# One mLSTM head stage on TensorE, with and without the filler products between its heads

## The reference

```python
D = exp(log_D - max_log_D)                # log_D: sums of log forget gates + input gate, -inf above the diagonal
C = (q @ k.T) / sqrt(32) * D
h = C / (max(|sum(C)|, exp(-max_log_D)) + 1e-6) @ v
```

## Time and profile before

| | |
|---|---|
| median of 3 runs | 1674.55 us |
| profiled execution | 1677.74 us |
| its span, first to last instruction | 1676.0 us |
| mean granted TensorE clock | 0.901 |
| heads: first to last `weigh` | 88.1 to 267.7 us |
| TensorE, VectorE busy, whole span | 1346.0, 1241.5 us |

### The profile page before, as it was taken

One profiled execution on the slowest core, in us unless ns is written; L12 is line 12 of the kernel. 1 busy time (PEld: TensorE's weight loads), 2 busy tenths in 40 slices (PEclk: granted clock), 3 DMA queues, 4 the chain that ended last, 5 costly groups with the idle time before them and its releaser, 6 DMA issues. The chain is left out here.

```text
span 1676.0 us, 24635 instructions
## 1 busy us (share of the span) xinstructions
PE 1346.0 (80%) x8976; PEld 758.8 (45%) x9000; DVE 1241.5 (74%) x1952; ACT 767.8 (46%) x1451; POOL 325.5 (19%) x233
## 2 busy tenths in 40 slices
PE   5599993636868989873967759679999999999996
PEld 3378773212334444432645546334444444444443
DVE  5567777825558778956999999488877777887764
ACT  3445562715334444424978879323333334433322
POOL 0032424607445557531000000000000000000000
PEclk8789996558888999996979889789999999999998
DMA  8312231355142242226030000000000000000000
GB/s 290 117 52 61 102 101 41 128 147 157 55 131 83 90 124 88 101 67 247 3 125 0 25 0 0 1 1 7 6 6 13 6 6 6 6 6 9 10 6 13
DMA packets 56493, 102.17 MB, mean 61 GB/s; under 512 B 9823, under 2 KB 20727, under 8 KB 56300
## 3 DMA queue, kind: packets, MB, share of 16 engines
q1 hardware_dynamic: 55148, 97.14, 17.5%
q0 software_dynamic: 1280, 4.20, 0.9%
HBM read 73.47 MB, written 27.66 MB: 60 GB/s over the span
## 5 line engine op out<-in xcount | busy, mean ns | idle before, releaser
L2084 PE MATMUL HG<-W1H,XT 128*128 128x512 f16 x512 | 166.6, 387 | 27.2 <-ACT XT L2045 20.7
L1558 PE MATMUL FD<-W0D,HH 128*128 128x512 f16 x512 | 159.6, 395 | 14.8 <-DMA W0D<-down_weights,IDX 12.2
L2084 PE MATMUL HU<-W1H,XT 128*128 128x512 f16 x512 | 163.2, 380 | 0.0
L2110 PE MATMUL HD<-W1H,HT 128*128 128x512 f16 x512 | 155.2, 380 | 0.0
L1552 PE MATMUL FG<-F,W0G 97*128 97x512 f16 x324 | 86.1, 400 | 52.9 <-DMA F<-features_kept 24.5
L2053 ACT ACTIVATE SG<-HG,DS 128x512 f32<-128x512 f32 x64 | 43.9, 686 | 160.6 <-PE HU L2084 160.6
L1805 ACT ACTIVATE PR<-A_S,NM,CM 128x512 f32<-128x512 f32 x128 | 99.5, 777 | 34.2 <-DVE NM L1946 34.2
L2187 DVE SCALAR_TENSOR_TENSOR H<-HU,DS,SG 128x512 f32<-128x512 f32 x64 | 48.0, 750 | 87.6 <-ACT SG L2053 85.7
L1442 POOL TENSOR_TENSOR HL<-HM,HH 128x512 f16<-128x512 f32 x64 | 92.3, 1442 | 86.0 <-ACT HH L1481 85.5
L335 ACT ACTIVATE DD<-E,TM 128x128 f32<-128x128 f32 x256 | 72.7, 369 | 70.3 <-PE E L431 68.7
L1558 PE MATMUL FD<-W0D,HL 128*128 128x512 f16 x256 | 100.1, 391 | 0.0
(11 more groups left out here) (335 smaller groups left out, 3369.8 us busy)
## 6 DMA issues: line engine op xcount, KB each, us to landing
VALP<-in_ffn_weights_dram SPq DMA_DIRECT2D x24, 512.0 KB, 3.6
VALQ<-in_ffn_weights_dram SPq DMA_DIRECT2D x24, 512.0 KB, 3.6
quantised_weights<-QQ SPq DMA_DIRECT2D x24, 512.0 KB, 2.8
X<-in_x_dram SPq DMA_DIRECT2D x8, 1024.0 KB, 6.0
CTX<-in_ctx_dram SPq DMA_DIRECT2D x8, 1024.0 KB, 5.6
W1H<-quantised_weights SPq DMA_DIRECT2D x3, 2048.0 KB, 10.6
W1L<-quantised_weights SPq DMA_DIRECT2D x3, 2048.0 KB, 15.4
F<-features_kept SPq DMA_DIRECT2D x16, 288.0 KB
```

Of the source, the lines that this page charges most:

```text
L1558: last = pe.matmul(DN[c][:, :], lhs[:, i, c * P:(c + 1) * P], W2[:, i, part, :], start=(i == 0 and n == 0), stop=(i == KI - 1 and n == 2))
L2084: ins = pe.matmul(bank[:, :], lhs, rhs, start=(i == 0), stop=(i == len(terms) - 1))
L2110: ins = pe.matmul(DN[0][:, :], HT[:, q, lp, k, :], W[:, 2, i * D:(i + 1) * D], start=(i == 0 and lp == 0 and W is WH), stop=(i == KI - 1 a ...
```

## The change

The function `fill` and its five calls go, which are 73 filler products between the heads. The twelve in front of the first head stay, and so does everything else, the order of the other products included.

```diff
-            def fill(n):
-                if n < HEADS:
-                    if n >= 2:
-                        pe.wait_ge(d_ready, n - 1)
-                    keep_warm(1, E[n % 2])
-
             def decay(n):
...
                         i += 1
-                    if c == 2 and n:
-                        fill(HG * n + HG)
                 last.then_inc(state_ready, 1)
...
                 if pair % 2 == 0:
                     read_state(pair // 2)
-                    fill(ahead + 1)
                 if pair + 1 < HEADS // 2:
                     scores(pair + 1)
                 weigh(2 * pair + 1)
-                fill(ahead + 1)
                 decay(ahead + 1)
                 if pair % 2 == 1 and pair + 1 < HEADS // 2:
-                    fill(ahead + 2)
                     state(pair // 2 + 1)
```

## The result

The kernel after the change takes 1683.33 us, the median of 20 runs (1673.88 to 1704.36), against 1676.23 us for the kernel before (20 runs, 1672.37 to 1683.17). The ratio is 1.0044, 95% interval 1.0024 to 1.0063: 7.4 us slower, between 4 and 11. The forecast was 1685. Every ratio here compares whole sets of runs, lies near the quotient of their means and not of the medians (these differ by 7.1 us), and leaves out runs over 1.5% above the fastest of their kernel, which are one of the twenty after the change and three of the six of `rows32`.

What follows compares the result with a forecast made beforehand. TensorE, busy 80% of the span, and its granted clock were taken as the bounds. Direct saving -7.5 us and further clock falls +18 us gave +10.5 us on 1674.55, so 1685 us; range 1665 to 1712 us.

Steps and rivals of the forecast that it cites:

- 43 fillers are on its path, 30 in a wait: In the heads, 43 fillers cost TensorE 0.22 us each, 9.5 us; the other 30 only fill a wait for CC.
- I take 0: For the 30 fillers in the wait for CC: of their 6.6 us, nothing is gained by dropping them.
- The direct part: Time saved in the heads by dropping the fillers, clock aside: 9.5 less 2.0, so -7.5 us, between 0 and -16.1.
- The square roots' waits: Three TensorE waits, once each in sequences 1 to 3, grow from 0.90 to some 1.6 us; 2.0 us not gained.
- Four further falls of the clock: In the heads, lighter runs without fillers drop TensorE's clock in a quarter of the groups: +18 us.
- 4.5 us for a fall: Price of one drop to half clock in the heads: 10.20 us holding 5.7 us of full-clock work.
- the first stay: Half-clock stretch from 95.6 to 105.8 us, expected to remain; change in its length taken as 0, at most 7.4 us more.
- the clock's part: Time lost in the heads by further drops to half clock: +18 us.
- the rival of the swinging clock: In the heads, about six or more falls, or falls outlasting a group: 1694 to 1719 us, taken at 1704; chance 0.24.
- The rival of the clock that holds: No further falls in the heads, only the direct saving: 1667 us, or 1658 if all 16.1 are gained; chance 0.20.

Runs made afterwards that it cites:

- rows32: Kernel before with all 73 fillers kept, each using 32 rows of the array in place of 128: 1768.36 us, ratio 1.0484.
- rows64: Kernel before with all 73 fillers kept, each using 64 rows of the array in place of 128: 1782.89 us (4 runs, no ratio).
- start_30_root: Kernel before, fillers doubled up to head 9, then only the 30 in the wait for CC, plus six per square-root wait: 1666.63 us, ratio 0.9956.

## Why the prediction was right, point by point

- *TensorE sets the pace; 43 fillers are on its path, 30 in a wait.* Right. Groups at full clock: 10.80 us with all, 10.16 without the path's, 10.67 without the wait's, 10.03 with none, 11.87 with all doubled. The step "I take 0" for the 30 was 0.13 us per group too low, some 2 us over the stage. The direct part was about -9.5 us and not -7.5.
- *The square roots' waits grow by what goes in front of them.* Right: 0.90 to 1.55 us, and no gain there.
- *Four further falls of the clock.* The profiled run has four. Three stand where they were expected: behind scores, `weigh`, decay, `weigh` at 225.4 us, behind the same kinds at 153.7 us, and at 170.8 us, 1.9 us after a square root's wait. The fourth, at 194.7 us, followed a wait that I hadn't named (below). Four was a choice, and that it was met in one traced run is luck; this run confirms only the order. Over the 20 runs after the change the time rises with the time at half clock (correlation 0.88). The mean clock of the heads was 0.85, as forecast.
- *4.5 us for a fall.* The stays were 3.4, 13.7, 3.4 and 27.3 us, not 10 each; that their mean, 12 us, is near is luck. At 0.44 they cost 21.0 us against 18, and the first stay, 6.8 us in place of 10.2, gave 1.5 us of it back, where I had taken 0. So the clock's part was 1.5 us too small and the direct gain 2 us too small; these two errors nearly cancel. The term that was mis-sized is the length of a stay. Whether length or count makes the spread of the runs (1674 to 1704 us) is open, for only one has a trace. That a stay may outlast a group was in the rival of the swinging clock; it happened once in this run, with a group of 18.2 us wholly at half clock (230.72 to 248.89 us, state to state) where 17.5 had been worked out.
- *The rival of the clock that holds* is refuted: the fall at 225.4 us has no gap over 1.55 us in front of it, and `rows64` stayed at half clock for 228.6 us with no gap. The rule of the Trainium skill (page "TensorE: Matmul & The Clock Gate", section "Why this matters for your kernels"), which asks only for no long idle gaps, fails here with it. Where the clock does hold without the path's fillers (`start_30_root`), the time is about what that rival gave, 1667 us, though there the spared first stay is part of it.
- *The difference.* +7.4 us by the ratio (+7.1 by the medians) against +10.5 forecast. The 2 us of the direct part account for most of it; the rest is inside the interval. The absolute time came nearer, 1683.3 against 1685, because the three runs that the forecast started from (1674.55) lie 1.7 us below the median of the twenty.

## What to carry to other kernels

A filler product has a cost and a use that are to be read apart: its cost is the start-to-start time only where nothing hides it, its use is the time at half clock that it spares. Dropping the fillers on the path and dropping those in a wait brought as much half clock here, so put them into waits that another engine causes, where they cost next to nothing, and more of them where the trace shows the first fall (here the start of the stage). Look at what stands in front of each fall of the granted clock, and don't take a busy TensorE for a sign that the clock holds. A filler with a part of the rows is no substitute for a full one.

## What the runs showed of the hardware that I had not expected

- Fillers with 32 or 64 of 128 rows are worse than none: 1768 and 1783 us against 1683. At full clock a 32-row or 64-row one took 0.32 us from start to start, a 128-row one 0.22.
- Half clock can last while TensorE is busy throughout: with all fillers partial, it stayed at 0.50 for 71.7 us (32 rows) and 228.6 us (64 rows) in one piece.
- In the kernel after, one small VectorE step was held up beside a GpSimd copy, and a stay at half clock followed. The summary of that line (min/median/max ns), VectorE's step and what it delayed on TensorE, and the GpSimd copy beside it:

```profile
L600 DVE TENSOR_SCALAR DN<-DN x4: 194/194/1819, 141.0 to 284.7; 128x64 f32<-128x64 f32 x4
```

```profile
190.41 1.82 DVE L600 TENSOR_SCALAR DN<-DN 128x64 f32<-128x64 f32 x1
...
193.60 1.08 PE L436 MATMUL O<-VA,CC 128*128 128x33 f32 x8 [1.28 <-DVE CC L670]
```

```profile
190.29 1.90 POOL L216 COPY VA<-CTX 128x2048 f32<-128x2048 f32 x1
```

The step ended at 192.23 us, the copy at 192.19. TensorE then waited 1.28 us for CC, and the clock was at half from 194.7 us. That this wait brought the fall about is likely but not shown: falls came at such places without it too. The Trainium skill, page "SBUF — State Buffer", section "Who interferes with whom", says that such a VectorE operation can need a port that GpSimd holds and then blocks until GpSimd's instruction is done; the trace agrees. Before the change the same step took 0.195 us all four times: a shift in time made the two meet.
